# Convolution edge stages of a four-layer graph network: a deeper step pipeline, other PSUM banks, GpSimd written out, paired half-array matmuls

## What is computed

```python
h = silu(edge_scalars @ fc_w1 / sqrt(8))            # hidden, 64 wide
weight = h @ fc_w2 / sqrt(64)                       # 192 wide: w1, w2, w3, w4
f_s, f_v = x_s @ lin1_w0, x_v @ lin1_w1             # per node, gathered per edge
m0a = f_s[src] * y0 * w1;   m0b = sum(f_v[src] * y1) / sqrt(3) * w4
m1a = f_s[src] * y1 * w2;   m1b = f_v[src] * y0 * w3
mid = segment_sum(concat(m0a, m0b, m1a, m1b), dst)  # per target node
conv = (mid_s @ lin2_w0, mid_v @ lin2_w1)
out = layernorm(cos(angle) * self_connection(x) + sin(angle) * conv)
```

## Time and profile before

| | us |
|---|---|
| median of three runs | 5562.64 |
| profiled execution, its own time | 5514.92 |
| span of the profile, first to last instruction | 5513.0 |
| edge stage of layer 0, first use of a gathered row to the last scatter | 203 to 863 |
| edge stage of layer 2, first gather to the last scatter | 3437 to 4092 |
| edge stage of layer 3, likewise | 4405 to 5054 |
| busy PE, DVE, ACT, POOL | 4147.5, 3527.4, 2340.3, 3407.0 |

### The profile page before, as it was taken

The page is one execution under the profiler, slowest core; times in us unless marked ns, Lnnn a source line. Parts: engine busy times, 40 slices in busy tenths (PEclk is TensorE's granted clock), DMA queues, the critical chain, the costliest instruction groups (busy, mean ns, idle before and its releaser), DMA issues. The chain is left out here.

```text
span 5513.0 us, 73349 instructions
## 1 busy us (share of the span) xinstructions
PE 4147.5 (75%) x14102; PEld 1964.5 (36%) x14102; DVE 3527.4 (64%) x8554; ACT 2340.3 (42%) x6704; POOL 3407.0 (62%) x3639
## 2 busy tenths in 40 slices
PE   0499996775888877888888700888889788887777
PEld 0133334553232323323333300333347533333554
DVE  1466667996656555556655487455549945555999
ACT  0123324554433333333333166433449933333555
POOL 0266667998455544555554244666658866666988
PEclk9999997787878777787777655899989989998777
DMA  8222225665333333333333199222249822224775
GB/s 356 88 68 68 68 66 175 214 215 159 83 88 87 85 82 77 85 87 88 87 86 80 33 366 334 63 67 68 66 124 356 308 63 68 68 67 114 221 218 186
DMA packets 593199, 727.86 MB, mean 132 GB/s; under 512 B 80518, under 2 KB 410650, under 8 KB 592980
## 3 DMA queue, kind: packets, MB, share of 16 engines
q1 hardware_dynamic: 499688, 545.80, 32.7%
q0 software_dynamic: 86400, 142.71, 9.5%
q10 hardware_dynamic: 7020, 38.40, 1.7%
HBM read 498.42 MB, written 245.90 MB: 135 GB/s over the span
## 5 line engine op out<-in xcount | busy, mean ns | idle before, releaser
L548 POOL DMA_INDIRECT aggregates<-agg_out,scatter_index x600 | 615.0, 1025 | 402.6 <-issue 254.8
L1289 ACT ACTIVATE y_chunk<-residual,ln_minus_mean_rstd,ln_rstd 128x160 f32<-128x160 f32 x1568 | 693.1, 529 | 302.4 <-POOL ln_minus_mean_rstd L1352 217.7
L853 POOL TENSOR_TENSOR edge_ln_rstd<-edge_ln_var,minus_half 128x16 f32<-128x16 f32 x50 | 146.9, 2938 | 677.9 <-DVE edge_ln_var L1118 677.9
L1255 PE MATMUL psum<-self_weights,x_chunk_T 128*128 128x160 f32 (+1 forms) x2352 | 492.8, 361 | 66.5 <-ACT x_chunk_T L1302 30.5
L1348 POOL TENSOR_TENSOR ln_rstd<-ln_var_eps,minus_half 128x4 f32<-128x4 f32 x392 | 441.6, 1127 | 143.5 <-DVE ln_var_eps L1437 84.8
L624 PE MATMUL psum<-identity,scaled_x 128*128 128x128 f32 x600 | 145.0, 280 | 497.0 <-DVE scaled_x L698 311.3
L531 POOL DMA_INDIRECT gathered<-x_layer,gather_index x400 | 397.7, 994 | 176.2 <-issue 115.3
L1255 PEld LDWEIGHTS psum<-self_weights,x_chunk_T 128*128 128x128 f32 x2352 | 405.8, 220 | 127.7 <-issue 62.9
L1445 DVE BATCH_NORM_STATS2 ln_stats<-residual 128x6 f32<-128x160 f32 x1568 | 389.2, 307 | 0.1
L531 POOL DMA_INDIRECT gathered<-in_x,gather_index x200 | 207.3, 1036 | 209.8 <-DVE scaled_x L698 122.5
L570 ACT ACTIVATE scaled_x<-gathered,sh_times_attr 128x160 f32<-128x160 f32 x400 | 138.4, 417 | 460.2 <-DVE sh_times_attr L681 307.8
(11 more groups left out here) (221 smaller groups left out, 11274.0 us busy)
## 6 DMA issues: line engine op xcount, KB each, us to landing
x_layer<-y_chunk SPq DMA_DIRECT2D x294, 320.0 KB, 5.2
x_chunk<-x_layer SPq DMA_DIRECT2D x294, 320.0 KB, 4.7
agg_chunk<-aggregates SPq DMA_DIRECT2D x196, 320.0 KB, 5.4
sh_rows<-in_sh_big SPq DMA_DIRECT2D x50, 768.0 KB
agg_chunk<-aggregates SPq DMA_DIRECT2D x98, 384.0 KB, 6.0
aggregates<-agg_out ACTq DMA_DIRECT2D x48, 768.0 KB
x_chunk<-in_x SPq DMA_DIRECT2D x98, 322.0 KB, 3.0
agg_chunk<-aggregates SPq DMA_DIRECT2D x98, 322.0 KB, 3.7
```

Of the source, the lines that this page charges most:

```text
L548: eng.indirect_dma_start(agg_table[:, :], bass.IndirectOffsetOnAxis(idx_last[:, q, b:b + 1], 0), agg_out[:, q, b, :], None, bounds_check=N ...
L1255: eng.matmul(o[:, b, 0:ns + 96], x_t[:, k4, (2 * half + b) * 128:(2 * half + b) * 128 + 128], self_w[:, k, 0:ns + 96], start=b == 0, stop= ...
L1289: op = eng.activation(y_out[:, buf, b, :], res[:, buf, b, :], ACT.Identity, bias=shift[:, buf, b:b + 1], scale=rstd[:, buf, b:b + 1])
```

## The change

Seven things are changed, all in the convolution edge stages but the last:

1. The links of a group's chain lie in other steps. PE does in step s: T and F1 of group s-1, W and E of s-2, A of s-3, R of s-4. ACT does xt of s-1, w of s-2, hid of s-1, scale of s, agg of s-4. DVE does scale of s, P of s-2, V of s-3, agg of s-4. A stage has six last steps instead of three.
2. Banks: W1 and W2 share OS and OV2 with the projections A1 and B1, and R shares E1 and E2. TA and TB hold transposes alone. The waits go with that: W waits for the first segment sum of s-4, A1 waits for the copy w of s-2, E waits for agg of s-5, R waits for P of s-2.
3. POOL is written out without a loop, and takes its indices straight from `src_index` and `last_index`: the copies to `gather_index` and `scatter_index` and the waits around them are gone. It scatters group s-6 in step s.
4. F1 has its 64 columns twice, so `hidden` has 128 rows, and W1 takes the lower 64 rows of hidden and of the array, W2 the upper 64.
5. A1 takes only the upper 64 rows of `prod[:, 0]`, B1 only the lower 64, one after the other. (The other halves of these weights are zeros.)
6. The DMA of `sh_rows` is issued two steps later, under semaphores of its own.
7. In the setup SP issues eight small DMAs (the doubled weights and a bias) ahead of the others, and DVE waits for them before it scales weights.

The tiles `xt1`, `xt2`, `hid`, `w_sb` and `prod` still exist once.

```diff
+            eng.wait_ge(P["weights_in"], 64)
+            for layer in CONV:
+                fc1, fc2 = BLOCKS.index((layer, "F1")) * 128, BLOCKS.index((layer, "W2")) * 128
+                eng.dma_start(W(layer, "F1")[0:16, 64:128], t["weights"][0:16, fc1:fc1 + 64]).then_inc(P["self_in"], 16)
+                eng.dma_start(W(layer, "W2")[64:128, :], t["weights"][0:64, fc2:fc2 + 128]).then_inc(P["self_in"], 16)
+            for half in (0, 64):
+                eng.dma_start(b1_col[half:half + 64, :], t["small"][0:64, SM["b1"]:SM["b1"] + 2]).then_inc(P["self_in"], 16)
...
             eng.wait_ge(P["weights_in"], 64)
+            eng.wait_ge(P["self_in"], 16 * (T + 2) * len(SELF) + 128)
...
-        W1, W2, R0 = TA, TB, OS
+        W1, W2, R0 = OS, OV2, E1
+
+        def steps_c(eng, body):
+            steps(eng, NG, body, lead=6, lag=6)
...
-            def step(s, par):
-                held(eng, N - 1)
+            for s in range(NG + 6):
+                par = s % 2
                 if live(s, 0, NG):
...
-                    eng.tensor_copy(idx_src[:, par, :], src_i[:, bass.ds(g * T, T)]).then_inc(S["index"], 1)
...
+                    wait(eng, S["xs_act"], s - 1)
+                    wait(eng, S["xq"], s - 1)
+                    wait(eng, S["xa"], s - 1)
                     for b in range(T):
+                        col = s * T + b
                         eng.indirect_dma_start(gathered[:, par, b, 0:width], None, x_table[l][:, :],
-                                               bass.IndirectOffsetOnAxis(idx_src[:, par, b:b + 1], 0))\
+                                               bass.IndirectOffsetOnAxis(src_i[:, col:col + 1], 0))\
                            .then_inc(S["gather1"] if par else S["gather0"], 16)
-                if live(s, 3, NG):
...
-                    eng.tensor_copy(idx_last[:, q, :], last_i[:, bass.ds(g * T, T)]).then_inc(S["index_used"], 1)
...
+                if live(s, 6, NG):
+                    g = s - 6
...
+                    wait(eng, S["agg"], g + 1)
...
                 if live(s, 2, NG):
                     g = s - 2
+                    eng.wait_ge(S["hidden"], at(S["hidden"], g + 1))
+                    wait(eng, S["scan_s"], g - 1)
+                    wait(eng, S["vec_y"], g - 1)
+                    eng.matmul(bank(W1), W(l, "W1")[0:64, :], hid[0:64, :], start=True, stop=True)
+                    eng.matmul(bank(W2), W(l, "W2")[64:128, :], hid[64:128, :], start=True, stop=True)\
+                       .then_inc(S["w_mm"], 1)
+                    eng.wait_ge(S["xt_copied"], at(S["xt_copied"], g + 1))
+                    wait(eng, S["products"], g)
+                    wait(eng, S["agg"], g - 2)
+                    eng.matmul(bank(E1), W(l, "E1"), xt1[:, :], start=True, stop=True)
+                    eng.matmul(bank(E2), W(l, "E2"), xt2[:, :], start=True, stop=True).then_inc(S["e_mm"], 1)
+                if live(s, 3, NG):
+                    g = s - 3
                     eng.wait_ge(S["products"], at(S["products"], g + 1))
                     wait(eng, S["vec_m"], g)
                     eng.matmul(bank(OV3, 96), W(l, "B2")[:, 0:96], prod[:, 1, :], start=True, stop=True)
-                    wait(eng, S["agg"], g)
-                    eng.matmul(bank(OS, rows_s), W(l, "A1")[:, 0:rows_s], prod[:, 0, :], start=True, stop=False)
+                    wait(eng, S["w_copied"], min(g + 2, NG) if isinstance(g, int) else g + 2)
+                    eng.matmul(bank(OS, rows_s), W(l, "A1")[64:128, 0:rows_s], prod[64:128, 0, :], start=True, stop=False)
+                    eng.matmul(bank(OV2, 96), W(l, "B1")[0:64, 0:96], prod[0:64, 0, :], start=True, stop=True)
...
+                if live(s, 4, NG):
+                    g = s - 4
                     eng.wait_ge(S["scan_s"], at(S["scan_s"], g + 1))
                     eng.wait_ge(S["scan_v"], at(S["scan_v"], g + 1))
+                    eng.wait_ge(S["products"], at(S["products"], min(g + 3, NG) if isinstance(g, int) else g + 3))
+                    wait(eng, S["agg"], g)
...
                 if live(s, 2, NG):
                     g = s - 2
+                    eng.wait_ge(S["w_copied"], at(S["w_copied"], g + 1))
+                    eng.wait_ge(S["e_mm"], at(S["e_mm"], g + 1))
+                    wait(eng, S["proj"], g)
+                    eng.tensor_tensor(prod[:, 0, :], w_sb[:, 0, :], bank(E1), ALU.mult)
+                    eng.tensor_tensor(prod[:, 1, :], w_sb[:, 1, :], bank(E2), ALU.mult).then_inc(S["products"], 1)
```

More of the change, by code:

```diff
@@ L604, in step @@
                     op.then_inc(S["agg"], 1)
-            steps(eng, NG, step)
+            steps_c(eng, step)
         def edge_tensor(eng, l):
@@ L626, in step @@
                     op.then_inc(S["transposed"], 1)
-                    wait(eng, S["attr1"] if q else S["attr0"], (g - q) * 16 + 32)
+                    wait(eng, S["attr1"] if q else S["attr0"], (g - q) * 8 + 16)
                     wait(eng, S["hidden"], g)
-                    eng.matmul(bank(H, 64), W(l, "F1")[0:C["K"], 0:64], attr_t[0:C["K"], q, :], start=True, stop=True)\
+                    eng.matmul(bank(H), W(l, "F1")[0:C["K"], :], attr_t[0:C["K"], q, :], start=True, stop=True)\
                        .then_inc(S["hidden_mm"], 1)
```

147 lines of the change are left out of this document (58 added, 89 removed).

## The result

| | before | after |
|---|---|---|
| median, runs of one comparison | 5551.64 us | 5931.56 us |
| ratio, with its 95% interval | | 1.072 (1.059 to 1.085) |
| span of the profile | 5513.0 | 5909.2 |
| step of layer 0, 2, 3 | 12.77, 12.52, 12.45 | 16.04, 14.03, 13.26 |
| granted clock in these stages, windows of the earlier trace rows and below | 0.94, 0.91, 0.90 | 0.75, 0.84, 0.85 |

The account below looks back on a forecast made before the run. POOL was taken to bound the kernel before, the ring of waits after. Layers 0, 2, 3 at +65, -22, -28 and setup +5 make +20 on 5514.9: 5535 us; with 48 us to the median, 5583, range 5490 to 5690.

Parts of the forecast that it names:

- POOL sets the steps of before: Edge stages before: POOL's eight indirect DMAs and two index copies set steps of 12.77, 12.52, 12.45 us; 10.6 without copies.
- no real wait: POOL before, layer 2 gathers: its own issue and copies ended 57.4 and 20.5 of 80.4 us of idle time.
- Who waits in the new order: Edge stages after: single tiles close a ring of waits E, xt, w, A, P, R, T, F1, W inside each step.
- the ring at full clock: Edge stages after: the ring's links sum to 13.75 us in layer 0, 11.57 in layer 2, 11.39 in layer 3.
- Rival 3: Edge stages: POOL still sets the step, as the ring overlaps more; up to 300 us gained, 5260 us; chance 0.06.
- rival 4: Edge stages: paired matmuls don't run together, each pair costs 0.86 us more; +215, 5798 us; chance 0.04.
- The clock: PE in edge stages: granted 0.94, adding 0.32 us a step in layer 0, 0.50 in others; steps 14.07, 12.07, 11.89.
- Rival 2: PE in edge stages: half clock far more often, granted 0.85; steps 14.63, 12.94, 12.76; +135, 5698 us; chance 0.2.
- R, T, F1 and W fit beside V and agg (3.7 beside 5.25): Layer 0: these PE links, 3.7 us, run beside DVE's V and agg, 5.25 us, so stay outside the ring's sum.
- The skill's rule: PE's clock: by the page, scattered pauses are no cure and a less busy PE sees the lower clock more often.
- Filling and draining: Stage starts and ends: three more thin last steps, but first steps lack A and R; 0, with 10 us either way.
- Setup: Ahead of the first step: SP's eight more DMAs at 1.1 us each, 9 us at most; 5 taken.

Follow-up runs that it names:

- d4_pairs: Kernel before with only the paired half-array matmuls and their setup; POOL, links, banks and waits as before: ratio 0.998.
- d2_fill: Changed kernel with one matmul added in each PE pause (B2 twice, one ahead of R, in layer 0 one ahead of E): 5517.16 us, ratio 1.003 to before.
- d2_after: The changed kernel itself, run again on a chip with few late updates: 5719.70 us, ratio 1.040 to the kernel before.
- c1_before: The kernel before, unchanged, as a control on a third chip: ratio 1.0004.
- e1_fill: Changed kernel with more matmuls in PE's pauses (B2 three times, three ahead of R, in layer 0 three ahead of E): 5972.60 us, ratio 1.080 to before.
- e2_swap: Changed kernel with ACT copying w ahead of xt: 5841.54 us, ratio 1.056 to the kernel before.
- d3_two: Changed kernel with ACT copying w ahead of xt and two sets of `prod`, without added matmuls: 5287.07 us, ratio 0.961 to before.
- e8_fill_small: Changed kernel with one matmul added in each PE pause, on a second chip: 5517.99 us, ratio 1.012 to the kernel before.

## Why the prediction was wrong, by its own steps

*POOL sets the steps of before*: right in the main. With less work on POOL they fall by 0.9 to 1.0 us, with less on PE (`d4_pairs`) by 0.15 at most, and behind POOL the next limit stands at 11.5 to 11.9. But "no real wait" was read from the gathers. Ahead of the scatters POOL did wait for agg, in layer 0 for 31.0 us in 262 to 820, 0.7 a step:

```profile
L548 POOL DMA_INDIRECT aggregates<-agg_out,scatter_index x173 | 178.9, 1034 | 101.7 <-issue 69.4 <-DVE agg_out L745 31.0 <-DVE scaled_x L698 1.2
```

*Who waits in the new order, and the ring at full clock*: right, within 0.25 us. 13.75, 11.57, 11.39 forecast; 13.51, 11.59, 11.63 in `d2_fill` (R to R at full clock 13.7 to 13.9 in layer 0, in `d2_after` 11.8 to 12.0 and 11.5 to 11.7). The pairs run at the same time. Rival 3 (POOL still the bound) and rival 4 fall.

*The clock*: the step that failed. I took 0.94, the highest of the three clocks of before, because one pause of 1.47 us did no harm. After, two pauses of 1.3 to 1.7 us stand in nearly every step, and the clock was 0.75 to 0.76 in layer 0 in all three profiles of this kernel, 0.85 to 0.87 in layer 3. The steps of layers 0 and 3 came out 2.0 and 1.4 us over the forecast, on chips without late updates 1.9 and 1.0 to 1.2. One pause was a poor guide: in this same layer 3 of before, 4450 to 5020 us, PE waits at this place 32 times, 2.05 us in the mean, and the clock of the stage was 0.90:

```profile
PE psum L647 <- ACT hidden L582: 65.7, 32, 3.8
```

Filling the pauses took 2.5 us and 1.25 us off these two, on one chip: 16.02 to 13.51 and 12.88 to 11.63. Rival 2 had the mechanism, but also its size too small: it divided only 4.96 us by the clock in layer 0, which gives 15.4 even at 0.75.

That is a second fault in the same step. "R, T, F1 and W fit beside V and agg (3.7 beside 5.25)" holds at full clock only. In the step shown, R, T, F1 and W take 618.81 - 611.85 = 7.0 us. They then are the longer way, and the ring is PE's: 10.2 + 6.8 = 17.0 instead of 13.75. A chain's bound has to be worked out anew at the lower clock, not divided by it.

*The skill's rule*: the Trainium skill (TensorE: Matmul & The Clock Gate, Part 1) has the throttled state as the default, which I had weighed and set aside for the row with 1.47. The traces here agree with the page in layer 0: 0.76 with the pauses, 0.99 with most of each filled. Layer 2 of `d2_after`, 0.97 with the pauses, does not bear out the forecast drawn from it.

*Layer 2*: on chips without late updates 11.72 and 11.78 us at a clock of 0.98 and 0.97, forecast 12.07. In the profile after it was 14.03. Between the two stand late updates, 32% against 0%, and a clock of 0.84; which of them led to the other is not shown.

*Filling and draining*: 0 with 10 us either way was wrong. From `c1_before` to `d2_after` the stages grew by more than their 50 steps: layer 0 by 181.7 us, first use of a gathered row to last scatter, of which 50 x (16.02 - 12.88) = 157 are steps; 21 and 21 more in the others the same way. The filling, the three more steps at the end and their effect on the mean step come to some 67 us together.

*Setup*: 9.8 us until the first gather (83.4 after 73.6), where I took 5 of at most 9.

*The last node stage*, which is not changed, took 459.9 us in the profile of before and 514.7 in that of after. It is 508.4 in `c1_before` and 509 to 516 in all the others, so nearly all of its 55 us is no price of the change.

*The chip*: 1.072 in the result, 1.040 and 1.043 on chips without late updates. So some 3 points of the 7 go with the chip of the result, and what holds PE's updates up there is open.

The sum for the profiled execution, forecast 5535: steps 50 x (1.97 + 1.96 + 1.37) = 265; filling and draining 26 + 21 + 21, the stage lengths less 50 steps; setup 5; last node stage 55; the stretch of attention between the edge stages -15: 5913, and the profile after has 5911.1.

## What to carry to other kernels

Write down the ring of waits that a reordering closes, then sum it twice, at full and at half clock: PE's links that are hidden at the one may set the step at the other, and short pauses in every step can bring the half clock about (layer 0 here; layer 2 kept 0.97 with them). If buffers exist once, cut the ring first (a second set, another order of two copies) before moving links. Profile both kernels on one chip. And take apart a change of several parts: here POOL's form and the pairs are worth 4.5%, and the moved links with their banks, which look like the main part, lose 8.5.

## What was not expected of the hardware

**Chips differ in how soon PE's updates are seen.** Late updates of the edge stages were 0% on three chips, 0 to 3% on a fourth, and 25 to 49% on a fifth, but for layer 0 of `e1_fill` (0%) and `e2_swap` (9%); the profiles of the result had 4 to 6% before and 6, 32 and 24% after. ACT's were never late in these stages. Between chips the ratio of one program to the kernel before moved by 4% (POOL alone 1.020 and 0.977; the program of `d3_two` 1.0005 and 0.961), and by 0.9% between two chips without late updates (`e8_fill_small` 1.012, `d2_fill` 1.003). The stretch from the edge stage of layer 0 to that of layer 2, which no run changes, took 2486 to 2500 us on the three chips, 2571 on the fourth, 2616 to 2622 on the fifth, 2575 and 2560 in the profiles of the result. The traces with late updates also hold fewer records of updates (225 against 277 in layer 2 of the changed kernel), so the shares are rough. Each chip was used once, so chip and occasion are not told apart. What holds the updates up isn't known.

**The last node stage has two lengths for the same code**, 460 and some 510 us. In the groups of that stretch, of the profile of before,

```profile
L1289 ACT ACTIVATE y_chunk<-residual,ln_minus_mean_rstd,ln_rstd 128x160 f32<-128x160 f32 x392 | 171.4, 508 | 6.0 <-POOL ln_minus_mean_rstd L1352 6.0
...
L1348 POOL TENSOR_TENSOR ln_rstd<-ln_var_eps,minus_half 128x4 f32<-128x4 f32 x98 | 100.3, 1023 | 0.5 <-DVE ln_var_eps L1437 0.4
```

and of `c1_before`, the same program:

```profile
L1289 ACT ACTIVATE y_chunk<-residual,ln_minus_mean_rstd,ln_rstd 128x160 f32<-128x160 f32 x392 | 171.4, 508 | 75.5 <-POOL ln_minus_mean_rstd L1352 75.5
...
L1348 POOL TENSOR_TENSOR ln_rstd<-ln_var_eps,minus_half 128x4 f32<-128x4 f32 x98 | 143.6, 1465 | 0.5 <-DVE ln_var_eps L1437 0.4
```

the small POOL operation takes 1.02 or 1.47 us, and ACT waits for the one that follows it on POOL (L1352). What makes it longer was not looked for; that DVE and POOL meet at the memory is only argued. The Trainium skill says that they share their interface to it (GPSIMD Engine Reference, Specifications).

**The clock is not a function of the pause alone.** Layers 2 and 3 of `d2_after` have the same ring but for w, which is longer by 0.18 us in layer 2, and pauses up to 1.8 and 1.7 us in nearly every step, and 0.97 against 0.87. Why is open.
